# Unread products of the identity on TensorE, in the last sliding steps and in the pauses between four stages

## What is computed

```python
h = mamba_block(x)      # in_proj, conv, a scan over 2048 rows with 16 states, out_proj, an MLP
h = moe_block(h)        # 8 experts, the best 2 of each row, and a shared expert of 256
h = sliding_block(h)    # 16 heads of 16, each row attends to the 128 rows up to its own
y = routed_block(h)     # light attention in windows of 64 (8 heads of 64), two routings of
                        # 50 coordinate-descent iterations, heavy attention on the routed rows
```

```python
scores = einsum('bhcid,bhcjd->bhcij', q_chunk, k_two_chunks) / sqrt(16)   # 128 x 256 a chunk
scores = where(band, scores, -inf)
attn = softmax(scores); out = einsum('bhcij,bhcjd->bhcid', attn, v_two_chunks)
```

## Time and profile before

| | |
|---|---|
| time, median of 3 runs | 2540.46 us (2535.93 to 2549.74) |
| time of the profiled execution | 2543.61 us |
| its span | 2541.9 us |
| TensorE busy | 2261.9 us, 89% of the span |
| DVE, ACT, POOL busy | 75%, 59%, 52% |
| mean granted clock of TensorE | 0.943 of the full one |
| first three stages end for TensorE at | 1042.1, 1461.4 and 1881.4 us |

### The profile page before, as it was taken

The page is one execution under the profiler, slowest core; times in us unless marked ns, Lnnn a source line. Parts: engine busy times, 40 slices in busy tenths (PEclk is TensorE's granted clock), DMA queues, the critical chain, the costliest instruction groups (busy, mean ns, idle before and its releaser), DMA issues. The chain is left out here.

```text
span 2541.9 us, 48920 instructions
## 1 busy us (share of the span) xinstructions
PE 2261.9 (89%) x17037; PEld 1586.3 (62%) x17037; DVE 1907.5 (75%) x4315; ACT 1507.2 (59%) x3369; POOL 1332.4 (52%) x1277
## 2 busy tenths in 40 slices
PE   5879999999999888799999979999878998999797
PEld 2555656565666555577787746666645776777555
DVE  5999999999999995367667458788845555566545
ACT  6778888888888864333333334554535667655522
POOL 2887979797878884233333224554553332321411
PEclk8979999999999998899999979999958999999898
DMA  6545444444544441100000234334120000000300
GB/s 208 165 139 170 151 152 160 142 164 137 167 139 163 137 146 54 50 30 1 1 1 1 51 80 77 73 56 69 36 78 2 21 23 19 18 19 19 113 15 9
DMA packets 139509, 206.87 MB, mean 81 GB/s; under 512 B 24481, under 2 KB 59426, under 8 KB 139138
## 3 DMA queue, kind: packets, MB, share of 16 engines
q1 hardware_dynamic: 137282, 200.86, 27.2%
q0 software_dynamic: 960, 2.62, 0.3%
q10 hardware_dynamic: 1024, 0.26, 0.1%
HBM read 161.42 MB, written 14.68 MB: 69 GB/s over the span
## 5 line engine op out<-in xcount | busy, mean ns | idle before, releaser
L534 POOL TENSOR_TENSOR ma_seen<-ma_state,ma_cs 128x1024 f32<-128x1024 f32 x256 | 602.7, 2366 | 179.8 <-DVE ma_state L1301 166.1
L1301 DVE TENSOR_TENSOR_SCAN ma_state<-ma_decay,ma_last,ma_drive 128x512 f32<-128x512 f32 x512 | 626.0, 1262 | 4.9 <-ACT ma_decay L1049 4.9
L1049 ACT ACTIVATE ma_decay<-ma_dt,ma_a_neg 128x512 f32<-128x512 f32 x512 | 338.7, 711 | 0.8 <-DVE ma_dt L1391 0.6
L1288 DVE TENSOR_TENSOR ma_drive<-ma_weight,ma_bs 128x512 f32<-128x512 f32 x512 | 325.6, 681 | 0.0
L770 PEld LDWEIGHTS ma_acc<-ident,ma_seen 128*128 128x128 f32 x2048 | 244.6, 147 | 114.8 <-POOL ma_seen L534 61.4
L770 PE MATMUL ma_acc<-ident,ma_seen 128*128 128x128 f32 x2048 | 273.7, 283 | 44.5 <-POOL ma_seen L534 44.4
L2453 DVE CUSTOM_DVE_ANT_0 sw_score<-sw_score,both_band 128x256 f32<-128x256 f32 (+1 forms) x512 | 197.2, 446 | 55.2 <-PE sw_score L2267 44.3
L2391 ACT ACTIVATE sw_prob<-sw_turned 128x512 f32<-128x512 f32 (+1 forms) x256 | 135.5, 581 | 172.6 <-PE sw_turned L2281 150.7
L104 POOL TENSOR_TENSOR moe_h_low<-both_V,light_wqkv 128x512 fp32r<-128x512 f32 x80 | 104.9, 1312 | 245.8 <-DVE light_wqkv L100 238.4
L2189 POOL TENSOR_SCALAR_AFFINE_SELECT sw_prob<-sw_prob 128x512 f32<-128x512 f32 x128 | 84.5, 660 | 202.5 <-ACT sw_prob L2391 202.5
L1913 DVE TENSOR_TENSOR both_V<-both_V,moe_up 128x512 f32<-128x512 f32 x80 | 55.0, 687 | 119.1 <-PE moe_up L1702 73.8
(11 more groups left out here) (596 smaller groups left out, 5715.9 us busy)
## 6 DMA issues: line engine op xcount, KB each, us to landing
ma_bs<-bc_rows SPq DMA_DIRECT2D x256, 256.0 KB, 3.3
ma_cs<-bc_rows SPq DMA_DIRECT2D x256, 256.0 KB, 3.3
ma_h<-kept_taps SPq DMA_DIRECT2D x28, 256.0 KB, 4.3
both_wide<-both_kh SPq DMA_DIRECT2D x28, 192.0 KB, 4.6
both_wide<-both_qh SPq DMA_DIRECT2D x20, 256.0 KB, 4.6
x_rows<-X SPq DMA_DIRECT2D x1, 4096.0 KB, 14.3
light_rows<-li_y SPq DMA_DIRECT2D x32, 128.0 KB, 1.7
out_dram<-li_o SPq DMA_DIRECT2D x32, 128.0 KB, 1.8
```

The costliest lines, as they stand in the source:

```text
L534: g.tensor_tensor(out=seen[n % RR][:, :, :], in0=state[n % SR][:, :, :], in1=each(cs[n % CR][:, :], 2), op=ALU.mult).then_inc(S["seen_full ...
L1049: a.activation(decay[s % DR][:, :], dt[:, m, :], ACT.Exp, scale=a_neg[:, m, k:k + 1]).then_inc(S["decay_done"], 1)
L1288: v.tensor_tensor(out=drive[mm][:, :], in0=weight[mm][:, :], in1=bs[n % CR][:, :], op=ALU.mult).then_inc(S["drive_done"], 1)
L1301: v.tensor_tensor_scan(state[n % SR][:, mm, :], decay[s % DR][:, :], drive[mm][:, :], last[:, k, m:m + 1], ALU.mult, ALU.add).then_inc(S[" ...
```

## The change

`run_in` multiplies the identity with itself a given number of times, into a PSUM tile that nobody reads afterwards. It is called at six places, all on TensorE: 26 times at the end of the mamba stage, 30 times at the end of the experts' stage, once in each round of the last 8 sliding steps (between the wait for `exped` and the first product of `shifted`), 22 times at the end of the sliding stage, and 6 and 12 times in the opening of the last stage, behind the transpose L3284 and behind the product L3287. It waits for nothing and no semaphore is added. Nothing is removed or moved, and the other engines' programs are as before. Line numbers of the kernel after are 8 higher behind the new function, and higher still behind each call.

```diff
+def run_in(t, out, ident, times):
+    for _ in range(times):
+        t.matmul(out[:, 0:P], ident[:, :], ident[:, :], start=True, stop=True)
...
             for j in range(GT):
                 outputs(LAST, j)
+            run_in(t, acc, K["ident"], 26)
...
                 for unit in moe_extras(i, n):
                     extra(*unit)
+            run_in(t, gate[0], K["ident"], 30)
...
                 since(pe, "exped", 2 * R)
+                if n >= STEPS - 8:
+                    run_in(t, turned[0], K["ident"], 1)
                 for e in range(2):
...
                     if r == 3 and 0 <= n - 1 < STEPS:
                         front(n - 1)
+            run_in(t, score[0], K["ident"], 22)
...
             t.transpose(tops, part[:, :], K["ident"][:, :]).then_inc(S["max_turned"], 1)
+            run_in(t, outT, K["ident"], 6)
             pe.wait_ge(S["max_diag"], 1)
             pe.wait_ge(S["made"], made_steps[0])
             t.matmul(small, ones[0:PROBLEMS, :], diag[:, :], start=True, stop=True).then_inc(S["max_spread"], 1)
+            run_in(t, outT, K["ident"], 12)
```

## The result

The changed kernel takes 2546.75 us (median of 19 runs, 2534.58 to 2552.83). The kernel before, run beside it, takes 2536.01 us (19 runs, 2532.06 to 2550.58). The ratio is 1.0031, with a 95% interval of 1.0015 to 1.0046: a loss of 0.3% (4 to 12 us), where 0.4% less was forecast. It is within the 0.5% named as no change, but clear in sign, and 2546.75 lies outside the range of 2523 to 2541.

A forecast was written before the change was run, and what follows sets the result against it. TensorE, busy for 89% of the span at a mean clock of 0.943, was taken as the bound. Terms of +0.4 - 2.5 + 1.3 - 1.3 - 8.5 + 1.0 - 2.8 = -12.4 took 2543.6 to 2531.2 us, range 2523 to 2541.

The forecast's parts named there:

- the part on steps 24 to 28: Sliding steps at full clock: products delay by 1.3 us, and an avoided clock fall at 1820.5 gives 1.3 us back.
- enough to hide 0.22 in about half of the rounds: Sliding steps: TensorE's 6.5 us in 12 waits for DVE over 55 us hide the product in half the rounds.
- one 0.22 a step, 1.3 us in six steps: Sliding steps: the unhidden products delay each step by one product, +1.3 us in all.
- all four rounds would be 5: Sliding steps: the delay in us over six steps if the product were on the path in all four rounds.
- The last rounds: -8.5: Last ten rounds of exponentials from 1840.9: full clock instead of half saves 8.5 us, bounds -2 to -10.7.
- End of the first stage, +0.4: Pause after the first stage: 26 products make the barrier 0.4 us later, full clock gives nothing back; bounds 0 to +0.4.
- End of the second stage, -2.5: Pause and sliding stage's start: 30 products cause no delay, full clock starts DVE 2.5 us earlier; bounds 0 to -2.6.
- End of the third stage, +1.0: Pause from 1881.4: 22 products end 0.5 us late, part possibly at half clock; 1.0 us later taken.
- Opening, -2.8: Last stage's opening: full clock for eight transposes and eight projections saves 2.8 us, bounds +1.2 to -3.3.
- The products run at half clock: Rival, 6%: clock already fallen when runs of products start, delays at stage ends and last rounds, no gain; 2562 us.
- More comes back: Rival, 22%: half-clock stretches elsewhere shift favourably and another 4 to 6 us go; 2526 us.
- transposes or identities don't count as work: Two rivals on the clock: identity products don't count, 4%, 2555 us; transposes don't, 3%, half the opening's gain lost, 2532 us.

The follow-up runs named there:

- control2: The kernel before with no edit, run again for its trace: 2534.96 us at a mean clock of 0.947.
- again: The changed kernel with no further edit, run again: 2545.33 us, ratio 1.0015 to the kernel before.
- narrow: The changed kernel with the round's product given only 32 columns of weights: 2545.56 us, ratio 1.0026 to the kernel before.
- turnings: The changed kernel with transposes of the identity for products, one in a round, two for each at the stage ends: 2543.86 us, ratio 0.9995 to the kernel before.
- tail: The changed kernel with the round's product only in the last seven rounds, where no scores are left: 2539.35 us, ratio 0.9999 to the kernel before.
- two: The changed kernel with two products instead of one in each of the 32 rounds: 2550.11 us, ratio 1.0052 to the kernel before.
- opening: The changed kernel with only the 22 products at the third stage's end and the last stage's 6 and 12: 2545.61 us, ratio 1.0002 to the kernel before.
- control3: The kernel before with no edit, once more for its trace: 2553.53 us at a mean clock of 0.938.
- allsteps: The changed kernel with the product in every round of all 32 sliding steps: 2577.85 us, ratio 1.0154 to the kernel before.
- rounds: The changed kernel with only the product in the rounds kept, none at stage ends or opening: 2546.86 us, ratio 1.0013 to the kernel before.

## Why the prediction was wrong

**The step that failed is in the part on steps 24 to 28: "enough to hide 0.22 in about half of the rounds", and with it "one 0.22 a step, 1.3 us in six steps".** The product was priced at 0.22 us from products standing in a row. Between `scores` and `shifted` it takes 0.51. Four a step are 2.0 us, and TensorE's waits for DVE in the earlier trace rows, 6.5 us in 55, are 1.1 a step: the rest, 0.9 us a step, is on the path. The two windows show it, 62.8 against 56.7 us for steps 24 to 29: 6.1 us instead of 1.3. The prediction's own "all four rounds would be 5" was nearer. It named as its own disproof a growth of over 0.5 us a step, and also a run of identities of more than 7 us, which came too (8.49 us, at the second stage's end).

The price of 0.51 could have been read from the trace of before. The products of 48 and 49 rows stand in turn on the rows from 0 and from 64 (`slice(64 * s, 64 * s + SROWS)`), and the trace has them start in pairs, 0.003 us apart; a full-height product takes the rows of both. By the starts of single instructions, in the median of 22 rounds of `control2` and of 13 rounds of the first trace alike, it is 0.12 us from the last product of `scores` to the first of `shifted`, but 0.20 from the last of `shifted` to the first of `mixes`, which has 128 rows. The added product puts two such changes into each round: 0.21 from `scores` to it, 0.21 between its two instructions, 0.21 from it to `shifted`, in place of the 0.12.

**The second: "The last rounds: -8.5".** Its mechanism held: the clock is 1.00 there, and the 18 exponentials take 21.6 instead of 26.7 us; ACT's wait for `shifted` fell from the 17.0 us of the earlier trace rows to 10.5 in the same window, with four more exponentials in it:

```profile
L2404 ACT ACTIVATE sw_prob<-sw_turned 128x512 f32<-128x512 f32 x24 | 13.0, 595 | 13.3 <-PE sw_turned L2293 10.5 <-PE sw_outT L2307 2.8
```

In the windows of 18 exponentials that is 5.1 us gained from a cold execution. But the gain was priced against one execution with 34 us at half clock, and others do without. The faster heap, some six of ten runs, is taken for these, which is inferred from the times. In `control2` the same 18 take 18.7 us, and the product makes them 2.9 us slower, since it stands on TensorE behind the wait for ACT and ahead of `shifted`, on the loop itself. The position of the profiled time in the upper part of the runs, 3.1 us above the median, was a hint, and was treated as an offset of the whole sum. Against `control2`, whose span is 8.7 us shorter, this stretch alone is 11.7 us longer.

**End of the first stage, +0.4:** 7.10 us against 6.65, and nothing came back. Right.

**End of the second stage, -2.5: right at the spot, gone later.** The first `high` of the queries starts 4.3 us after the first scores, where it was 6.9: 2.6 us gained. In the first profile 1.5 of it was lost at once, because the clock fell at 1462.4, inside the 30 products, which then took 8.49 us. And by step 24 nothing is left. From the first scores to the first exponential of step 24 the seven profiles with these products and none in the rounds before step 24 have 318.5 us in the mean (314.6 to 322.8), the six without 317.4 (315.8 to 319.8). In `again`, `narrow` and `turnings` the clock falls three times for 3.4 us in steps 17 to 22 (in `again` at 1701.8, 1715.5 and 1766.7), where the kernel before has none or one; but `tail` and `two` have none there. Whether the products earlier on cause such falls, or only the shifted phase does, 13 executions can't tell.

**End of the third stage, +1.0:** 6.46 us against 5.91, 0.55 late, with the clock at 1.00. **Opening, -2.8:** 3.1 us gained, 0.6 ahead of the projections and 2.6 in them, against this one execution; over the four profiles of the kernel before, whose first eight projections take 5.4 to 6.2 us, it is 2.8. Both right, with the price that `opening` and `turnings` show when the clock is down.

**The rivals.** "The products run at half clock" was given 6% as a case of everything at once; in truth it happens at single ends, in four of the nine profiles with products there (`tail` at two of them), for 0.7 to 1.6 us each. "More comes back" did not come. That transposes or identities don't count as work is not what the windows of `turnings` and of the change show. The real loss was not among the rivals: a price by neighbour, and a baseline that was worse than usual in just the place to be mended.

**The sum.** Against an execution of the kernel before without a fall, the change costs 9.0 us in its last 64 exponentials and 0.5 at each of two ends, and gives 3.1 back at the opening: +7. Against `control3`, the deepest fall of the four, it is 6.9 us faster in the stretch. Of the 79 runs of the kernel before in the three series of experiments (two far outside left out) 47 are below 2542 us and 22 above 2548. Weighed so (0.6 at 75.4, 0.3 at 91.3, 0.1 at 82.0, which is an estimate: which run has which stretch was seen in four profiles only), the stretch takes 80.8 us before and 84.4 after: +3.6, and with the ends and the opening +1.5. Measured were 4 to 12 us, and in `again` -2 to 10. In the first measurement, though, 15 of the 19 runs of the kernel before are below 2542 us and three above 2548. With these shares the stretch takes 78.3 us before, and the sum is +4.0, the lower edge of the 4 to 12 measured there. So a good part of the difference between the two measurements is how often the kernel before had its fall.

That the rounds' products cost 0.51 us each and 9.0 us in the stretch is shown by the traces, and `two` and `allsteps` are clear of the kernel before in time as well; `tail` agrees, but its ratio alone would not separate it from `again`. The second stage's end, which gives 2.6 us at the spot and nothing by step 24, is already counted at nothing. What stays open is up to 8 us of the first measurement, and what the nine runs of the changed kernel above 2548 us lose, since both of its profiles are of faster runs (2537.14 and 2541.68 us).

## What to carry to other kernels

Price an added instruction between the neighbours it will have, not in a row of its own kind: here it was 0.51 us against 0.22. Before a fall of the clock is worked on, look at it in several executions; what one profile shows at half clock may be absent in others. Work that only keeps the clock up is worth placing where the engine would stand idle anyway, and an engine that is busy for 49.1 of 56.7 us and gets 2 us more in each of six steps has no such place.

## What the runs showed of the hardware

**A change between half-height pairs and full height.** In the kernel before, the first load for `shifted` (49 rows) starts at 1794.79, 0.23 us after `scores` begin and 0.11 before its own first product. In the changed kernel the loads of L112 and of the `shifted` behind it start no sooner than their products:

```profile
1800.27 0.30 PEld L112 LDWEIGHTS sw_turned<-ident 128*128 128x128 f32 x2
...
1800.69 0.52 PEld L2293 LDWEIGHTS sw_turned<-both_QP,both_wide 49*128 49x128 f32 x8
```

So two loads that were hidden behind other products are in the open, one on each side of the full-height product. The Trainium skill (TensorE: Matmul & The Clock Gate, Part 2, Step-by-step: what each phase is for) says that the engine pulls a weight load ahead of running products when the row groups don't conflict or when the load goes to the background weight buffer. The traces agree that loads are pulled ahead, but not that a conflict of rows decides here: in the row of 26 products at the first stage's end each load of 128 rows starts 0.003 us behind the product before it, which uses the same rows and lasts 0.27 us, and the load of `shifted` in `control2` starts on the rows of a product of `scores` that has just begun. What is in the open is the load at a change between pairs on half of the rows and products on all of them. Each such change takes 0.20 to 0.21 us from start to start, in the kernel before (`shifted` to `mixes`) as in the changed one, against 0.11 to 0.12 within one kind; the first two instructions of the identity behind it are 0.21 apart as well. Why is not shown; a product of 49 rows in the same place was not run.

**The clock's falls move from one execution to the next of one kernel.** Over the stretch of 64 exponentials, four executions of the kernel before had a mean clock of 1.00, 0.88, 0.79 and 0.73 and took 74.7, 81.3, 86.4 and 90.6 us from the first start to the last end. With a product in each round, the three profiles that have it at full clock throughout (the changed kernel's two and that of `allsteps`) agree within 0.1 us, at 83.7; in `rounds` it falls all the same, to 0.86 over the last rounds. Where it held, the products bought an even time in this stretch, at the price of a worse best one.

**Transposes of the identity held the clock as its products did.** At the second stage's end 60 transposes took 6.71 us, all at 1.00, and the 60 instructions of 30 products 8.49 us with 3.4 us at half clock among them; both left the clock at 1.00 behind the stage's end.
